# One tiling for near and far scores in attention, with masks and second norms on GpSimd and V's differences and routing steps on VectorE

## Chip, cores and metric

One core of one Trainium2 chip. The metric is device time in microseconds of one execution of the whole program; lower is better.

## The reference

```python
mod = (_silu(L0_c) @ L0_wmod).reshape(L0_c.shape[0], 6, 1, -1)
sa, ca, ga, sb, cb, gb = (mod[:, 0], ...)
ga = (2 * (ga >= 0) - 1) * jnp.maximum(jnp.abs(ga), 0.25)      # gb likewise
h = _layernorm(x, axis=-1) * (1 + ca) + sa
# attention: 16 heads of 64, 4 KV heads, on 4 x 1024 tokens of 128 features
scores = SOFTCAP * jnp.tanh((q @ k) * SCALE / SOFTCAP)         # SOFTCAP 30
mask = (j <= i) & (j > i - WINDOW)                             # WINDOW 128
o = softmax(where(mask, scores, -1e30)) @ v
x = x + ga * (o @ Wo.T)
h = _layernorm(x, axis=-1) * (1 + cb) + sb
# mixture of 8 experts, top 1, capacity C = tokens / 8 = 512
idx = jnp.argmax(softmax(h @ Wg), axis=1); loc = cumsum(one_hot(idx)) - 1
hidden = relu(h[rows of e] @ W1[e] + b1[e]); out = gate * (hidden @ W2[e] + b2[e])
x = x + gb * out                                               # (loc < C only)
```

## The kernel before, in words

4 batches of 1,024 tokens are cut into 32 tiles of 128 tokens (`BATCH_TILES` 8); two tiles make a block. `x` is normalised, turned (`turn_x`), split into a high and a low part and projected to Q, K and V in three passes per product. A tile needs its own keys and those of the tile before it in its batch; the first tile of a batch (`first(t)`) has no earlier one.

`score(t, h)` (TensorE, L478 to L489) makes 8 heads at a time: the tile's own keys go to the PSUM tensor `own` (2 banks), the keys of the tile before to two banks of `turns` (6 banks), in 16 matmuls of 32 keys with 512 down to 128 columns. `merge` (VectorE, L1352) copies the earlier tile's scores over own's by the triangle `before`, since a query sees each key slot in one of the two tiles. `weigh` and `expose` (ScalarE, L988 and L994) take tanh and exp into `PR`. `mask` (GpSimd, L1987) keeps of `PR` the part that belongs to the own tile, in `PM`.

Attention is linear in V: out = PR x V(t-1) + PM x VD, with VD = V(t) - V(t-1), made by `differ` on GpSimd (L1977). `sums` (L543) multiplies PR by ones. `attend` takes PR by V(t-1) for the first 64 queries and by VM for the other 64 (L521, all 128 keys deep), then PM by VD (L530, 64 keys deep, two row halves at once). VM is half V(t) and half V(t-1); SyncE copies it with 56 DMAs (`mix_v`, L326). ScalarE copies V out of PSUM (`keep_v`, L968).

After that, per tile: VectorE turns and inverts the sums and scales the output in two halves (`scale`, L1385), ScalarE takes the high part `OH` (L1001), GpSimd the low part `OL` (`low_o`, L1996), TensorE projects out and turns (`out_project`, `turn_y`), VectorE adds x and takes the moments (`add_x`, `measure2`, `gather2`), GpSimd the reciprocal deviation (`rstd2_of`, L2001 and L2003), VectorE normalises, modulates and shifts (L1408, L1416, L1420). TensorE turns that row (`turn_h2`) and scores the experts; VectorE finds the best one; GpSimd marks it (`mark`, L2012), adds it to the experts' counts (`add_seen`, L2022), numbers the slot, names the row and scatters it by an indirect DMA to `sorted_rows` (`scatter`, L2041). TensorE counts (`count`, L589, L590) between these steps, and needs `seen` of the tile before.

The expert stage (`place`, L814, to the end) starts with the rows of the last tiles, puts 512 rows an expert through W1 and W2 and scatters into the output.

The order of each engine's work is written out by hand: a loop over pairs of tiles and a longer list at both ends. Each PSUM bank has a table of tenants (`HOME`, `HOME_AT_ENDS`), and a tenant waits until the one before is read. At the end of the attention stage `run_between` (L602) puts 15 matmuls on zeros, 4,736 columns in all, between TensorE's steps.

## Time and profile before

| | |
|---|---|
| Three runs | 439.87, 441.22 and 441.91 us, median 441.22 |
| The profiled execution | 439.5 us, its span 437.8 us |
| TensorE busy | 418.3 us, 96% |
| VectorE, ScalarE busy | 288.8 us (66%), 296.9 us (68%) |
| GpSimd busy | 311.4 us (71%) |
| Head, to the first score | 15.9 us |
| Score of tile 8, 24, 28 begins | 90.8, 260.2, 301.3 us |
| Scatter of tile 28's rows is issued | 362.8 us |
| Expert stage | 366.3 us to the end |

In the trace an f32 matmul leaves two records, so "x32" at L530 are 16 matmuls. The end of a matmul's record holds its drain through the array, so the step from start to start, and not the duration, is the time one takes among others. Idle time is given in brackets with what ended it.

### The profile page before, as it was taken

The numbers are of one execution on the slowest core, as the hardware profiler recorded it, in microseconds if no ns is written. First come the engines' busy times: TensorE is split into PE (matmuls) and PEld (weight loads), VectorE is DVE, ScalarE is ACT, GpSimd is POOL, SyncE is SP. The second block draws the span as 40 slices with busy tenths as digits, with TensorE's granted clock in tenths as the row PEclk, the third lists the DMA queues.
The fourth block names the chain that finished last, engine by engine and source line by source line (L and its number), as shares of the span: only waits on it lengthen the run. The fifth ranks groups of instructions, "written<-read, shape, count | busy, mean of one in ns | idle before, by whom it ended". The sixth has DMA issues, their size and how long they took to land. (4 is left out here: it accounts for less than half of the span.)

```text
span 437.8 us, 15112 instructions
## 1 busy us (share of the span) xinstructions
PE 418.3 (96%) x5676; PEld 302.2 (69%) x5676; DVE 288.8 (66%) x884; ACT 296.9 (68%) x541; POOL 311.4 (71%) x496
## 2 busy tenths in 40 slices
PE   8989999999999999999999999999998998999992
PEld 4846666757676767576777767777664664789992
DVE  6485567666867686668585857676777665386751
ACT  4897676878695959776877787777677433645540
POOL 4267565758496979787979795889889974266663
PEclk9999999999999999999999999999999999999997
DMA  8087603000111020111212210302041152695010
GB/s 248 7 285 264 220 1 87 8 14 9 32 27 52 25 87 15 39 34 68 65 36 51 88 50 1 98 22 98 22 123 33 38 182 91 206 371 194 31 43 29
DMA packets 33023, 37.15 MB, mean 85 GB/s; under 512 B 3650, under 2 KB 29255, under 8 KB 32952
## 3 DMA queue, kind: packets, MB, share of 16 engines
q1 hardware_dynamic: 29448, 27.43, 20.4%
q0 software_dynamic: 3072, 8.37, 5.2%
q8 instruction: 46, 0.75, 0.7%
q10 hardware_dynamic: 432, 0.40, 0.4%
q14 instruction: 25, 0.20, 0.1%
...
## 5 line engine op out<-in xcount | busy, mean ns | idle before, releaser
L1352 DVE COPY_PREDICATED own<-before,turns 128x1024 f32<-128x1024 uint32 x56 | 68.5, 1223 | 52.0 <-PE turns L489 51.8
L988 ACT ACTIVATE PR<-own 128x1024 f32<-128x1024 f32 x64 | 65.7, 1027 | 33.6 <-DVE own L1352 32.2
L1996 POOL TENSOR_TENSOR OL<-O,OH 128x512 fp32r<-128x512 f32 x64 | 82.3, 1289 | 2.4 <-PE turns L530 1.1
L1987 POOL TENSOR_SCALAR_AFFINE_SELECT PM<-PR 128x1024 f32<-128x1024 f32 x64 | 69.7, 1098 | 17.0 <-ACT PR L994 16.6
L994 ACT ACTIVATE PR<-PR 128x1024 f32<-128x1024 f32 x64 | 67.1, 1054 | 0.1
L485 PE MATMUL own<-Q,K 64*32 64x128 f32 (+3 forms) x896 | 58.2, 436 | 1.7 <-ACT PR L988 1.4
L489 PE MATMUL turns<-Q,K 64*32 64x256 f32 (+3 forms) x896 | 57.7, 429 | 0.0
L1385 DVE TENSOR_TENSOR O<-turns,R 128x512 f32<-128x512 f32 x64 | 42.2, 685 | 11.4 <-PE turns L530 10.5
L2041 POOL DMA_INDIRECT sorted_rows<-PAY,slot_i x32 | 34.0, 1064 | 15.3 <-issue 10.2
L1001 ACT ACTIVATE OH<-O 128x512 fp32r<-128x512 f32 x64 | 40.0, 629 | 4.9 <-DVE O L1385 4.9
L489 PEld LDWEIGHTS turns<-Q,K 64*32 64x32 f32 x896 | 36.4, 107 | 9.3
L974 ACT ACTIVATE Q<-turns 128x512 f32<-128x512 f32 x64 | 37.8, 597 | 7.4 <-PE turns L411 6.5
L409 PE MATMUL turns<-XH,WqH 128*128 128x256 f32 x128 | 39.2, 306 | 0.1
L2001 POOL TENSOR_SCALAR var<-mv 128x1 f32<-128x1 f32 x32 | 6.2, 192 | 43.6 <-DVE mv L1404 42.2
L411 PE MATMUL turns<-XH,WqL 128*128 128x256 f32 x128 | 35.9, 281 | 0.0
L410 PE MATMUL turns<-XL,WqH 128*128 128x256 f32 x128 | 35.9, 281 | 0.0
L521 PE MATMUL turns<-PR,V 128*32 128x256 f32 x448 | 34.7, 380 | 0.0
L521 PE MATMUL turns<-PR,VM 128*32 128x256 f32 x448 | 34.5, 379 | 0.0
L557 PE MATMUL turns<-OH,WoH 128*128 128x256 f32 x128 | 32.7, 294 | 0.0
L1281 ACT ACTIVATE PM<-turns,b_col 128x512 f32<-128x512 f32 x28 | 19.3, 688 | 19.2 <-PE turns L411 19.1
L543 PE MATMUL turns<-PR,ones 128*32 128x512 f32 x224 | 29.8, 604 | 1.7 <-ACT PR L994 0.8
L558 PE MATMUL turns<-OH,WoL 128*128 128x256 f32 x128 | 31.1, 281 | 0.0
...
## 6 DMA issues: line engine op xcount, KB each, us to landing
...
```

The source lines that it names most:

```text
L409: pe.matmul(dst, wh, xh, start=True, stop=False)
L485: pe.matmul(own[lo:lo + B, a, :].rearrange("p (r n) -> p r n", n=P)[:, :, lo:P], keys(a, t, lo, lo + B), q(a, lo, P), start=True, stop=Tru ...
L489: last = pe.matmul(ps[lo:lo + B, a, :].rearrange("p (r n) -> p r n", n=P)[:, :, 0:lo + B], keys(a, t - 1, lo, lo + B), q(a, 0, lo + B), st ...
L521: last = pe.matmul(out_of(c, x, g), v[:, d], probabilities(PM if first(t) else PR, slice(0, P), g, c), start=(x == 0), stop=(x == 1 and fi ...
L974: act.activation(Q[:, k % Q_RING, 2 * n:2 * n + 2, :], bank["q", k, n].rearrange("p (c n) -> p c n", c=2), ACT.Copy).then_inc(q_kept[n], 1)
L988: act.activation(pr, own[:, :, :].rearrange("p a n -> p (a n)"), ACT.Tanh, scale=SCORE_SCALE).then_inc(tanhed, 1)
L994: act.activation(pr, pr, ACT.Exp, scale=SOFTCAP).then_inc(exped, 1)
L1001: act.activation(OH[:, t % 2, :, half], O[:, t % 2, :, half], ACT.Copy).then_inc(oh_done, 1)
L1352: dve.copy_predicated(own[:, :, :].rearrange("p a (r n) -> p (a r) n", n=P), before[:, :].bitcast(U32).unsqueeze(1).to_broadcast([P, 2 * R ...
L1385: dve.tensor_tensor(O[:, t % 2, :, half].rearrange("p c (r n) -> p c r n", n=HALF), bank["pv", t][:, :, half].rearrange("p c (r n) -> p c ...
L1987: pool.affine_select(out=PM[:, u % P_RING, :].rearrange("p (r n) -> p r n", n=P), in_=PR[:, u % P_RING, :].rearrange("p (r n) -> p r n", n ...
L1996: pool.tensor_tensor(OL[:, t % 2, :, half], O[:, t % 2, :, half], OH[:, t % 2, :, half].bitcast(F32), ALU.subtract).then_inc(ol_done, 1)
```

## The change

**Scores.** The 128 x 128 keys and queries of a tile are cut into halves of 64. A far pair (early keys with late queries or late keys with early queries) belongs wholly to one of the two tiles, a near pair to both by a triangle. `own` is laid out as far, near, near, far, so the near parts are the middle 512 of 1,024 columns (`NEAR`). `score` issues 24 matmuls instead of 16 for a later tile (16 instead of 4 for a first one), with the same number of columns for a later tile. `merge` and `mask` treat 512 columns instead of 1,024. `mask` is now a multiply by a 0/1 table `visible`, built at the start with three more GpSimd operations.

**Attention.** `sums` and the first half of the products are one function `attend` (L508, L519, L525), the rest is `correct` (L543, L552). All of it works on 64 keys a matmul, two row halves at once: 64 matmuls of 256 columns a later tile. VM, `mix_v` and its 56 DMAs are gone. The sums take two banks; the products of every tile have the same two banks (4 and 5), where odd and even tiles had different ones.

**Engines.** `keep_v` goes from ScalarE to VectorE; `differ`, `mark`, `name_row` and `number_slot` go from GpSimd to VectorE. `normalise2`, `modulate2` and `shift2` go from VectorE to GpSimd and keep their value in SBUF (`normed2`, in a free part of PM).

**Order.** All lists are written anew: projections of Q are issued up to a block earlier, the routing steps later, and `run_between` has 21 matmuls with 7,552 columns in place of 15 with 4,736. ScalarE splits the first weight of Q before it normalises x.

```diff
-        before = sb("before", [P, P])
-        earlier = YT[:, 0:P]
...
+        before, visible = sb("before", [P, HALF]), sb("visible", [P, HALF])
...
+        normed2 = PM[:, P_RING - 1, 2 * REP * HALF:2 * REP * HALF + 2 * P].rearrange("p (t n) -> p t n", t=2)
...
+        NEAR, NEAR_KEPT = slice(REP * HALF, 3 * REP * HALF), slice(0, 2 * REP * HALF)
+        def near(a):
+            return slice((1 - a) * REP * HALF, (2 - a) * REP * HALF)
+        def far(a):
+            return slice(a * REP * HALF, (a + 1) * REP * HALF)
 
...
+                if not first(t):
+                    n, ps = take_two("before", t, h)
+                for lo in range(0, P, B):
+                    there = HALF - lo // HALF * HALF
+                    for a in range(2):
+                        pe.matmul(heads(own[lo:lo + B, a, far(a)]), keys(a, t if first(t) or lo < HALF else t - 1, lo),
+                                  q(a, there, there + HALF), start=True, stop=True, tile_position=(HALF * a, lo))
+                for lo in range(0, P, B):
+                    here, from_ = lo // HALF * HALF, 0 if first(t) else lo % HALF
+                    for a in range(2):
+                        last = pe.matmul(heads(own[lo:lo + B, a, near(a)])[:, :, from_:HALF], keys(a, t, lo),
+                                         q(a, here + from_, here + HALF), start=True, stop=True, tile_position=(HALF * a, lo))
...
+                for lo in (B, 3 * B, 0, 2 * B):
+                    here, to = lo // HALF * HALF, lo % HALF + B
                     for a in range(2):
...
+                        last = pe.matmul(heads(ps[lo:lo + B, a, near(a)])[:, :, 0:to], keys(a, t - 1, lo),
+                                         q(a, here, here + to), start=True, stop=True, tile_position=(HALF * a, lo))
...
+                n, sm = take_two("sums", t)
                 if first(t):
                     pe.wait_ge(masked, 2 * t + 2)
                 else:
                     pe.wait_ge(exped, 2 * t + 2)
...
+                    for half in range(2):
+                        last = pe.matmul(sm[32 * g:32 * g + 32, half, near(half)], ones32[HALVES[half], :],
+                                         near_m(t, g, half) if first(t) else near_p(PR, t, g, half),
+                                         start=True, stop=first(t) and half == 0, tile_position=(HALF * half, 32 * g))
+                last.then_inc(near_summed, 1)
+                m, ps = take_two("pv", t)
+                if t % 2 == 0:
+                    pe.wait_ge(v_kept, t // 2 + 1)
+                for x in range(2):
+                    for g in range(KV):
+                        d = slice(g * D + 32 * x, g * D + 32 * x + 32)
+                        for half in range(1 if first(t) else 2):
+                            last = pe.matmul(out_of(ps, 1 - half, x, g), V[HALVES[half], (t - half) % V_RING, d], far_p(t, g, half),
+                                      start=(x == 0), stop=False, tile_position=(HALF * half, 32 * g))
+                last.then_inc(far_done, 1)
+                pe.wait_ge(near_summed, t + 1)
+                for g in range(KV):
+                    for half in range(1 if first(t) else 2):
+                        last = pe.matmul(sm[32 * g:32 * g + 32, 1 - half, near(1 - half)], ones32[HALVES[half], :], far_p(t, g, half),
+                                         start=False, stop=True, tile_position=(HALF * half, 32 * g))
...
-                freed[n] = sums_turned, t + 1
+                freed[n] = freed[n + 1] = sums_turned, t + 1
+                freed[m] = freed[m + 1] = scaled, 2 * t + 2
...
+            def correct(t):
...
+                ps = bank["pv", t]
+                pe.wait_ge(far_done, t + 1)
+                if not first(t):
+                    for x in range(2):
+                        for g in range(KV):
+                            d = slice(g * D + 32 * x, g * D + 32 * x + 32)
+                            for half in range(2):
+                                pe.matmul(out_of(ps, half, x, g), V[HALVES[half], (t - 1) % V_RING, d], near_p(PR, t, g, half),
+                                          start=False, stop=False, tile_position=(HALF * half, 32 * g))
+                    pe.wait_ge(masked, 2 * t + 2)
+                    pe.wait_ge(vd_done, later_tiles(t) + 1)
+                for x in range(2):
+                    for g in range(KV):
+                        d = slice(g * D + 32 * x, g * D + 32 * x + 32)
+                        for half in range(2):
+                            v = V[HALVES[half], t % V_RING, d] if first(t) else VD[HALVES[half], t % VD_RING, d]
+                            last = pe.matmul(out_of(ps, half, x, g), v, near_m(t, g, half), start=first(t) and half == 0 and x == 0,
+                                             stop=(x == 1), tile_position=(HALF * half, 32 * g))
+                last.then_inc(pv_done, 1)
+
+            def out_of(ps, c, x, g):
+                return ps[32 * g:32 * g + 32, c, x * 2 * P:(x + 1) * 2 * P]
...
-                freed[n] = h2_done, t + 1
+                freed[n] = x1_done, t + 1
...
-                dve.copy_predicated(own[:, :, :].rearrange("p a (r n) -> p (a r) n", n=P),
-                                    before[:, :].bitcast(U32).unsqueeze(1).to_broadcast([P, 2 * REP, P]),
-                                    bank["before", t, h].rearrange("p a (r n) -> p (a r) n", n=P)).then_inc(merged, 1)
+                if t == 1 and h == 0:
+                    dve.wait_ge(consts, MASKS)
+                dve.copy_predicated(own[:, :, :].rearrange("p a n -> p (a n)")[:, NEAR].rearrange("p (r n) -> p r n", n=HALF),
+                                    before[:, :].bitcast(U32).unsqueeze(1).to_broadcast([P, 2 * REP, HALF]),
+                                    bank["before", t, h].rearrange("p a n -> p (a n)")[:, NEAR].rearrange("p (r n) -> p r n", n=HALF)).then_inc(merged, 1)
...
+            def keep_v(k):
+                dve.wait_ge(v_projected, k + 1)
+                if k >= 3:
+                    dve.wait_ge(pv_done, 2 * k - 3)
+                r = 2 * k % V_RING
+                dve.tensor_copy(V[:, r:r + 2, :], bank["v", k].rearrange("p (t n) -> p t n", t=2)).then_inc(v_kept, 1)
...
+                dve.wait_ge(v_projected, t // 2 + 1)
+                dve.wait_ge(v_kept, (t + 1) // 2)
+                if t >= VD_RING:
+                    dve.wait_ge(pv_done, t - VD_RING + 1)
+                now = bank["v", t // 2].rearrange("p (t n) -> p t n", t=2)[:, t % 2, :]
+                dve.tensor_tensor(VD[:, t % VD_RING, :], now, V[:, (t - 1) % V_RING, :], ALU.subtract).then_inc(vd_done, 1)
...
-                pool.affine_select(out=PM[:, u % P_RING, :].rearrange("p (r n) -> p r n", n=P),
-                                   in_=PR[:, u % P_RING, :].rearrange("p (r n) -> p r n", n=P), compare_op=ALU.is_ge, fill=0.0,
-                                   base=0, pattern=[[0, 2 * REP], [1, P]], channel_multiplier=-1).then_inc(masked, 1)
+                pool.tensor_tensor(PM[:, u % P_RING, NEAR_KEPT].rearrange("p (r n) -> p r n", n=HALF),
+                                  PR[:, u % P_RING, NEAR].rearrange("p (r n) -> p r n", n=HALF),
+                                  visible[:, :].unsqueeze(1).to_broadcast([P, 2 * REP, HALF]), ALU.mult).then_inc(masked, 1)
...
+            def normalise2(t):
+                pool.wait_ge(rstd2_done, t + 1)
+                if t >= 2:
+                    pool.wait_ge(h2_done, t - 1)
+                pool.tensor_scalar(normed2[:, t % 2, :], PAY[:, t % PAY_RING, ROW_X:ROW_X + P], mv2[:, t, 0:1], rstd2[:, t:t + 1],
+                                  ALU.subtract, ALU.mult).then_inc(n_done, 1)
+
+            def modulate2(t):
+                n = normed2[:, t % 2, :]
+                pool.wait_ge(n_done, t + 1)
+                if t == 0:
+                    pool.wait_ge(mod_in, 16)
+                pool.tensor_tensor(n, n, mod[:, t // BATCH_TILES, 1, :], ALU.mult).then_inc(m_done, 1)
+
+            def shift2(t):
+                pool.wait_ge(m_done, t + 1)
+                pool.tensor_tensor(PAY[:, t % PAY_RING, ROW_H:ROW_H + P], normed2[:, t % 2, :], mod[:, t // BATCH_TILES, 0, :],
+                                  ALU.add).then_inc(h2_done, 1)
+
...
```

TensorE, one later tile of the steady loop, before (`turns` holds the results, P is 128):

```order
L543 MATMUL turns<-PR,ones 32x512 x4
L521 MATMUL turns<-PR,V 32x256 x4
L521 MATMUL turns<-PR,VM 32x256 x4
L521 MATMUL turns<-PR,V 32x256 x4
L521 MATMUL turns<-PR,VM 32x256 x4
L530 MATMUL turns<-PM,VD 32x256 x16
```

and now, from the first sums to the end of the next score:

```order
L508 MATMUL turns<-PR,ones 32x256 x8
L519 MATMUL turns<-PR,V 32x256 x16
L525 MATMUL turns<-PR,ones 32x256 x8
L543 MATMUL turns<-PR,V 32x256 x16
L552 MATMUL turns<-PM,VD 32x256 x16
L468 MATMUL own<-Q,K 32x256 x8
L473 MATMUL own<-Q,K 32x256 x2
L473 MATMUL own<-Q,K 32x4x32 x2
L473 MATMUL own<-Q,K 32x256 x2
L473 MATMUL own<-Q,K 32x4x32 x2
L481 MATMUL turns<-Q,K 32x256 x4
L481 MATMUL turns<-Q,K 32x4x32 x4
```

The deep matmuls on all 128 keys are gone, and the score follows the products at once.

GpSimd, steady loop, before, from a mask to a scatter:

```order
L1987 AFFINE_SELECT PM<-PR 128x1024 x2
L1977 TENSOR_TENSOR VD<-V 128x256
L2028 COPY PAY<-tok_id 128x1
L1996 TENSOR_TENSOR OL<-O,OH 128x2x256
L1987 AFFINE_SELECT PM<-PR 128x1024
L1963 TENSOR_SCALAR var<-mv 128x2
L1964 TENSOR_SCALAR minus<-mv 128x2
L1966 TENSOR_TENSOR rstd<-var,neg_half 128x2
L1969 TENSOR_TENSOR shift<-minus,rstd 128x2
L2041 DMA sorted_rows<-PAY,slot_i 32768x388
```

and now:

```order
L1983 TENSOR_TENSOR PM<-PR,visible 128x512
L1997 TENSOR_SCALAR var<-mv 128x1
L1999 TENSOR_TENSOR rstd<-var,neg_half 128x1
L2029 TENSOR_TENSOR seen<-seen,onehot 128x8
L2042 DMA sorted_rows<-PAY,slot_i 32768x388
L2029 TENSOR_TENSOR seen<-seen,onehot 128x8
L2005 TENSOR_SCALAR PM<-PAY,mv,rstd 128x128 x2
L2013 TENSOR_TENSOR PM<-PM,mod 128x128
L2017 TENSOR_TENSOR PAY<-PM,mod 128x128
L1983 TENSOR_TENSOR PM<-PR,visible 128x512
L2013 TENSOR_TENSOR PM<-PM,mod 128x128
L1992 TENSOR_TENSOR OL<-O,OH 128x2x256 x3
```

The mask has two operands and half the columns; the norm's steps (L2005, L2013, L2017) stand where `differ` and the naming stood, between masks and low parts.

GpSimd, the last operations up to the scatter of tile 28 (the last row of each), before:

```order
L2022 TENSOR_TENSOR seen<-seen,onehot 128x8
L2001 TENSOR_SCALAR var<-mv 128x1
L2003 TENSOR_TENSOR rstd<-var,neg_half 128x1
L2016 CAST slot_i<-slot 128x1
L2001 TENSOR_SCALAR var<-mv 128x1
L2003 TENSOR_TENSOR rstd<-var,neg_half 128x1
L2012 TENSOR_SCALAR onehot<-iota,top_at 128x8
L2041 DMA sorted_rows<-PAY,slot_i 32768x388
L2016 CAST slot_i<-slot 128x1
L2041 DMA sorted_rows<-PAY,slot_i 32768x388
```

and now:

```order
L1997 TENSOR_SCALAR var<-mv 128x1
L1999 TENSOR_TENSOR rstd<-var,neg_half 128x1
L1997 TENSOR_SCALAR var<-mv 128x1
L1999 TENSOR_TENSOR rstd<-var,neg_half 128x1
L2005 TENSOR_SCALAR PM<-PAY,mv,rstd 128x128
L2042 DMA sorted_rows<-PAY,slot_i 32768x388
L2013 TENSOR_TENSOR PM<-PM,mod 128x128
L2005 TENSOR_SCALAR PM<-PAY,mv,rstd 128x128
L2017 TENSOR_TENSOR PAY<-PM,mod 128x128
L2029 TENSOR_TENSOR seen<-seen,onehot 128x8
L2042 DMA sorted_rows<-PAY,slot_i 32768x388
```

Norm steps of later tiles stand between the last scatters, the marks and slot numbers have left.

## Rows read from the trace of the kernel before

**Rows 1.** The page: busy us, share, instructions; granted clock in 40 slices, in tenths.
```profile
PE 418.3 (96%) x5676; PEld 302.2 (69%) x5676; DVE 288.8 (66%) x884; ACT 296.9 (68%) x541; POOL 311.4 (71%) x496
...
PEclk9999999999999999999999999999999999999997
```

**Rows 2.** Windows: busy us of each engine (instructions), clock, DMA share, GB/s.
```profile
90.80:260.20 169.40, 168.27 (x2616) 120.05 (x2608) 117.74 (x373) 129.30 (x240) 131.53 (x213) 1.00 0.15 43
...
301.30:362.80 61.50, 58.91 (x834) 39.99 (x819) 42.45 (x159) 35.74 (x77) 53.12 (x91) 1.00 0.27 88
```

**Rows 3.** Timeline of TensorE, one later tile: start us, us, engine, line, operation.
```profile
203.03 1.07 PE L543 MATMUL turns<-PR,ones 128*32 128x512 f32 x8
...
205.75 1.09 PE L530 MATMUL turns<-PM,VD 64*32 64x256 f32 x32
206.64 0.63 PE L485 MATMUL own<-Q,K 64*32 64x512 f32 x12
...
207.85 0.39 PE L409 MATMUL turns<-XH,WqH 128*128 128x256 f32 x1
208.07 0.28 PE L410 MATMUL turns<-XL,WqH 128*128 128x256 f32 x1
208.19 0.28 PE L411 MATMUL turns<-XH,WqL 128*128 128x256 f32 x1
```

**Rows 4.** Timeline of TensorE in the head, with the idle time before each.
```profile
29.27 0.65 PE L485 MATMUL own<-Q,K 64*32 64x512 f32 x12 [0.45 <-ACT PR L988]
...
31.41 1.06 PE L543 MATMUL turns<-PR,ones 128*32 128x512 f32 x8 [0.82 <-ACT PR L994]
33.44 0.65 PE L485 MATMUL own<-Q,K 64*32 64x512 f32 x12 [0.97 <-ACT PR L988]
```

**Rows 5.** Groups of GpSimd by form: count, busy us, mean ns, idle before.
```profile
L1996 POOL TENSOR_TENSOR OL<-O,OH 128x512 fp32r<-128x512 f32 x64 | 82.3, 1289 | 2.4 <-PE turns L530 1.1 <-ACT OH L1001 1.0
...
L2041 POOL DMA_INDIRECT sorted_rows<-PAY,slot_i x32 | 34.0, 1064 | 15.3 <-issue 10.2 <-DMA Q<-sorted_rows 3.1 <-ACT PAY L1025 1.2
L1977 POOL TENSOR_TENSOR VD<-V 128x256 f32<-128x256 f32 x28 | 20.7, 740 | 0.1
...
L2012 POOL TENSOR_SCALAR onehot<-iota,top_at 128x8 bf16<-128x8 f32 x32 | 11.1, 346 | 3.1 <-DVE top_at L1433 2.4
...
L1958 POOL CAST earlier_b<-YT 128x128 bf16<-128x128 f32 x1 | 0.3, 283 | 0.0
```

**Rows 6.** Timeline of GpSimd in the steady stretch.
```profile
200.57 0.19 POOL L2001 TENSOR_SCALAR var<-mv 128x1 f32<-128x1 f32 x1
...
201.40 1.09 POOL L1987 TENSOR_SCALAR_AFFINE_SELECT PM<-PR 128x1024 f32<-128x1024 f32 x1
...
207.72 1.29 POOL L1996 TENSOR_TENSOR OL<-O,OH 128x512 fp32r<-128x512 f32 x1
208.96 0.55 POOL L2022 TENSOR_TENSOR seen<-seen,onehot 128x8 bf16<-128x8 bf16 x2
209.46 2.15 POOL L1987 TENSOR_SCALAR_AFFINE_SELECT PM<-PR 128x1024 f32<-128x1024 f32 x2
```

**Rows 7.** Timelines of GpSimd (first two rows) and TensorE at the stage's end.
```profile
360.32 1.11 POOL L2041 DMA_INDIRECT sorted_rows<-PAY,slot_i  x1 [0.17 <-issue]
...
362.78 0.98 POOL L2041 DMA_INDIRECT sorted_rows<-PAY,slot_i  x1 [1.13 <-issue]
...
361.35 0.60 PE L602 MATMUL own<-zeros 128*128 128x256 f32 x2
...
364.43 0.17 PE L589 MATMUL turns<-onehot,earlier_b 128*128 128x8 bf16 x1 [0.92 <-POOL seen L2022]
```

**Rows 8.** Groups by form of VectorE and ScalarE.
```profile
L1352 DVE COPY_PREDICATED own<-before,turns 128x1024 f32<-128x1024 uint32 x56 | 68.5, 1223 | 52.0 <-PE turns L489 51.8
...
L1416 DVE TENSOR_TENSOR turns<-turns,mod 128x128 f32<-128x128 f32 x32 | 9.4, 294 | 0.6
...
L994 ACT ACTIVATE PR<-PR 128x1024 f32<-128x1024 f32 x64 | 67.1, 1054 | 0.1
```

1574 lines of the change are left out of this document (720 added, 854 removed).

## The prediction

> **What bounds the kernel now.** I read the page's first two parts for the shares, the windows by stage, the timeline of TensorE in one steady stretch and in the head, then GpSimd's groups and timeline, and last the two engines' timelines at the end of the attention stage. TensorE is busy 96% of the span and its granted clock is full in every slice but the last [rows 1]; no other engine is above 71%. In the eight middle pairs of tiles (90.8 to 260.2 us) TensorE is busy 168.27 of 169.40 us while GpSimd is busy 131.53, or 16.4 of 21.2 us a pair [rows 2]. So there a microsecond counts only if it is TensorE's. In the stretch from the score of tile 28 (301.3) to its scatter (362.8) that turns: TensorE is at 58.9 of 61.5, part of it filler on zeros, GpSimd at 53.1 [rows 2]. In its last part TensorE runs filler on zeros (361.35) and waits 0.92 us for GpSimd's `seen` (364.43) [rows 7]. The expert stage can't start before the last scatters of rows, and GpSimd issues those (tile 28's at 362.78 [rows 7]). TensorE therefore owns the time up to about tile 28, GpSimd's list of work from there to the scatter. The head has three short stalls, 0.45, 0.82 and 0.97 us, each on ScalarE's tanh or exp [rows 4].
>
> **TensorE.** The score moves the same columns as before (5,120 a half tile), in 24 matmuls in place of 16; I cost it at nothing, as all of them keep one 32-column shape and the 16 of now take 1.21 us (206.64 to 207.85) [rows 3]. Attention: sums and PR by V and VM 2.72 us (203.03 to 205.75), PM by VD 0.89 to 206.64, together 3.61 [rows 3]. The change makes all of it 64 matmuls of 256 columns on half the rows, the shape of PM by VD, of which 16 take 0.89 with the change of shape ahead of them; four such sets with one change of shape for all are about 3.47. That is 0.14 less a tile, 3.4 over the 24 later tiles before tile 28 (4 more follow). Bounds: four times 0.89 is 3.56, a gain of only 0.05 a tile; nothing below 4 x 0.86 is likely, since the columns stay. The first tile of each of 4 batches gains some 0.2 each, 0.8 together. Leaving the half-row shape costs too: the first projection after a score starts 0.22 us before the second (207.85, 208.07), the second 0.12 before the third [rows 3], so an entry costs 0.1. Counted in the two orders, attention and score now follow each other without other work between, which takes the runs of half-row work from 66 to 56 (-1.0), but the projections and transposes are spread over 61 runs in place of 36 (+2.5). Part of the two overlaps (a run left is a run entered), so I take the net by tile 28 as -2.6, between -4.5 and 0.
>
> **Head.** Three stalls of 2.2 us in all [rows 4] have more projections ahead of them in the new order; the first projection is perhaps 0.5 later, because ScalarE splits a query weight before it normalises. I take -1.0, between -2 and +1.
>
> Score(28,0) then starts 3.6 us sooner, at 297.7 in place of 301.3 (the start of the second window in [rows 2]).
>
> **VectorE, ScalarE, SyncE.** VectorE's merge does half of its 1,024 columns (1,223 ns, 56 times [rows 8]), about 34 us less. It takes on keep_v (16 copies of 512 columns), differ (28, on 256) and three small steps a tile, and gives away the norm's three steps (the second 294 ns a tile [rows 8]): its total falls rather than rises. ScalarE loses keep_v. The 56 VM copies by DMA go; TensorE's timeline shows no wait for one ahead of PR by VM (203.03 to 205.75 without a gap [rows 3]). All of this costs and gives nothing while these engines are at 66 to 68% [rows 1]. If that cover went (VectorE now stands between v's projection and attention), the late piece would be keep_v behind a merge, half a microsecond a pair.
>
> **GpSimd, the term that decides.** No row shows a mask as a multiply of 512 columns by two inputs. From below: today's one-input mask of 1,024 columns takes 1.07 (two in 2.15 [rows 6]). From above, and nearest: low_o, two inputs of 512 columns, 1,289 ns, 1.24 us from start to start [rows 5, 6]. I take 1.24, so +0.17 a mask, 4 a pair. The two-input steps of the norm on 128 columns: the line from low_o's 512 over differ's 256 (740 ns) gives 0.47, and from start to start a little less; I take 0.43. Its first step has one input and two scalars out of columns. From below: a cast of 128 columns, 283 ns. But mark, one input and one such scalar, takes 346 ns for 8 columns alone, where var with constants takes 0.19 for one [rows 5, 6], so such scalars cost; I take 0.45, with 0.28 and 0.60 as bounds. That makes 1.31 a tile. What leaves a pair: differ 1.75 x 0.7, mark 2 x 0.35 [rows 5], and two one-column steps a tile at 0.19, together 2.7. A pair gets 0.7 + 2.6 - 2.7 = +0.6 and stands at about 17 busy of 21.2: hidden, as long as its order lets it be.
>
> At the end it is not hidden. After mask(28,0) the changed list, counted in its order, holds, up to the scatter of tile 28, 12 low_o at 1.24 = 14.9, 7 masks at 1.24 = 8.7, 8 second rstd at 0.83 (200.57 to 201.40 [rows 6]) = 6.6, 12 add_seen at 0.25 (208.96 to 209.46 for two [rows 6]) = 3.0, 11 scatters at 1.06 plus 0.17 of issue [rows 5, 7] = 13.6, 9 normalise at 0.45 = 4.0 and 16 steps of modulate and shift at 0.43 = 6.9: 57.7 us. Ahead of it: score 1.21, merge 0.65 (half of 1,223 ns), tanh and exp 2.1 (1,024 columns as now, exp 1,054 ns [rows 8]), 0.35 of hops, 4.3 together, and mask(28,0) itself, 1.2. With 1.0 for one forced wait on ScalarE's OH, as today at the last tile, the stretch is 64.2 us, against 61.5 now (301.3 to 362.8, the second window of [rows 2]): +2.7. So scatter(28) comes at 297.7 + 64.2 = 361.9 in place of 362.8: -0.9. The marks on VectorE shorten the last routing chain by 0.3. The filler grows by 6 matmuls and 2,816 columns; one of 256 takes 0.60 us with its tail (361.35 [rows 7]), so eleven such are 6.6 at most and some 5 with the tails overlapped, in a stretch where TensorE waits anyway; costed at nothing, and a rival below if that is wrong.
>
> The sum: -3.6 + 2.7 - 0.3 = **-1.2 us** on the profiled execution, which took 439.5 us with a span of 437.8. The median of the three runs is 441.22, so the forecast is **440.0 us**. About 0.5% (2.2 us) is what a measurement of this kernel can tell from no change.
>
> The price of modulate and shift rests on the line through two GpSimd rows; VectorE's own modulate of 128 columns takes 294 ns [rows 8], so the line puts GpSimd at 1.5 times that. The Trainium skill, GPSIMD Engine Reference, section 4.1 (Engine selection), puts elementwise add and multiply on VectorE and calls GpSimd about twice as slow with two inputs, near line rate with one. It speaks against this change, which hands GpSimd three kinds of two-input work; rival D is what it would make of it.
>
> **Rivals.** (A) GpSimd's new steps are cheap or well covered: the multiply costs no more than 1.07 and the head's stalls vanish (-2.2). The end stretch falls by 8 x 0.17 = 1.4 and the start by 1.2 more, which gives 437.4; with normalise at 0.28 also, 9 x 0.17 less, 435.9. For it: GpSimd's prices for 128 columns are interpolated. Against: low_o is a close neighbour of the multiply. (B) Slower: GpSimd becomes the bound already in the steady pairs. Its list is in-order, with masks behind norms that wait for rstd and for the tile's sum, and pv has one pair of banks for both parities now, so an attend waits for the scale of the tile before. If such a wait is 0.3 us a pair, 14 pairs lose 4.2, the 3.6 of gain is gone, and the end stretch still costs its 2.7: 439.5 + 4.2 - 3.6 + 2.7 - 0.3 = 442.5, and on the median's scale 444.2; at 0.45 a pair 446.3. It decides as soon as score(28,0) gains less than 2.4 us, for then +2.7 - 0.3 outweighs it. For it: GpSimd goes from 71% to a longer list in the same span, and it is the only engine that TensorE's attention needs late. Against: today it idles 4.7 us a pair [rows 2]. (C) The change does not do what it says at the end: the longer filler, not GpSimd, holds back the last counts. Filler stands between count and transpose on TensorE, so half of its extra 5 us would show: 442.5. (D) GpSimd takes twice VectorE's time for the two-input steps of the norm: 16 x (2 x 0.294 - 0.43) = 2.5 more at the end, 442.5. This is the rule named above from section 4.1; for it speaks only that today's two-input rows there are wide ones.
>
> **How the numbers follow.** The forecast case has 0.37, with a range of its own of 437.5 to 442.5; A 0.23, B 0.22, C 0.10, D 0.08. Faster by over 0.5% (below 439.0): all of A and 0.14 of the forecast case, 0.37. Slower (above 443.4): B, 0.02 of C, 0.02 of D and 0.01 of the forecast case, 0.27. Between: 0.36. The range takes in A down to 434.5, for stalls smaller still, and B up to 446.
>
> **What would show it.** Score(28,0) near 297.7; attend and correct of one tile 3.47 from start to end; the mask's multiply at about 1,290 ns; the norm's three steps at 400 to 480 ns each; from score(28,0) to the scatter of tile 28 some 64 us, GpSimd busy over 90% of it; TensorE's longest waits for GpSimd. Wrong would be: stalls of TensorE in the steady pairs for PM, OL or pv's banks (B), a full TensorE up to the last count (C), or a stretch of 60 us (A).

## The result, and the profile after

The changed kernel took **475.25 us** (median of 4 runs, 471.96 to 479.49) against 440.7 for the kernel before, run beside it: **1.0757 times as long, 95% interval 1.0658 to 1.0855**. One of the four runs fell in the slow state; the ratio, here and below, compares the means of the fast runs alone, which is why it isn't the quotient of the medians. The forecast was 440.0, with a range of 434.5 to 446. The profiled execution took 471.96, its span is 470.1.

The page of the kernel after, its shares and its slices, against [rows 1]:

```profile
PE 428.4 (91%) x8472; PEld 348.5 (74%) x8472; DVE 305.2 (65%) x928; ACT 289.3 (62%) x525; POOL 336.5 (72%) x471
...
PE   7999979999999999989899999899597969999992
...
POOL 5545555878886978979796989688579886246664
PEclk8999989999999999999999999999799989999997
```

TensorE is no longer busy throughout: 91% in place of 96. The windows of after say where; the first is that of [rows 2], the second runs from the last tanh to the scatter of tile 28:

```profile
core 0: us, PE busy (x) PEld busy (x) DVE busy (x) ACT busy (x) POOL busy (x), PEclk, DMA share, GB/s
90.80:260.20 169.40, 160.70 (x3814) 134.87 (x3822) 121.53 (x362) 118.78 (x214) 136.34 (x187) 0.99 0.10 30
...
365.20:395.00 29.80, 24.66 (x229) 16.20 (x228) 9.86 (x70) 8.80 (x25) 24.59 (x37) 0.94 0.35 116
```

In the same 169.4 us TensorE idles 8.7 where it idled 1.1 before. To compare kernels I cut each span at five marks that all have: the start of ScalarE's tanh for tile 8 and for tile 24 (first halves), the last tanh (tile 31, second half), the start of tile 28's scatter, the end. Between the first two lie eight pairs of tiles. Times in us, of the profiled executions, as differences of marks rounded to 0.1:

| kernel | to tile 8 | eight pairs | to last tanh | to scatter(28) | to the end | span |
|---|---|---|---|---|---|---|
| before | 94.4 | 168.0 | 80.6 | 19.8 | 75.0 | 437.8 |
| after | 97.5 | 177.7 | 90.0 | 29.8 | 75.1 | 470.1 |
| difference | +3.1 | +9.7 | +9.4 | +10.0 | +0.1 | +32.3 |

The loss is thus in three stages of some 10 us each, with 3.1 more ahead of them, and not in the expert stage. The costliest groups of VectorE and GpSimd in the changed kernel name a first suspect; these are rows of the page:

```profile
L1992 POOL TENSOR_TENSOR OL<-O,OH 128x512 fp32r<-128x512 f32 x64 | 81.8, 1290 | 17.5 <-ACT OH L1017 16.6
L1983 POOL TENSOR_TENSOR PM<-PR,visible 128x512 f32<-128x512 f32 x64 | 81.4, 1280 | 17.1 <-ACT PR L1010 16.8
...
L1359 DVE COPY_PREDICATED own<-before,turns 128x512 f32<-128x512 uint32 x56 | 38.6, 690 | 31.5 <-PE turns L481 31.4
...
L1459 DVE TENSOR_SCALAR onehot<-iota,top_at 128x8 bf16<-128x8 f32 x32 | 41.7, 1303 | 0.1
```

L1459 is `mark`, a comparison of 8 columns that the change moved from GpSimd to VectorE. On GpSimd it was 346 ns; here its mean is 1,303. Its own view (minimum, median and maximum) shows that this isn't its work:

```profile
L1459 DVE TENSOR_SCALAR onehot<-iota,top_at x32: 190/540/6254, 117.1 to 399.1; 128x8 bf16<-128x8 f32 x32
```

The timelines of GpSimd, VectorE and TensorE in one steady stretch show what it waits for:

```profile
203.93 1.29 POOL L1992 TENSOR_TENSOR OL<-O,OH 128x512 fp32r<-128x512 f32 x1
205.18 2.50 POOL L1983 TENSOR_TENSOR PM<-PR,visible 128x512 f32<-128x512 f32 x2
...
204.70 3.02 DVE L1459 TENSOR_SCALAR onehot<-iota,top_at 128x8 bf16<-128x8 f32 x1
207.63 0.68 DVE L1359 COPY_PREDICATED own<-before,turns 128x512 f32<-128x512 uint32 x1
...
208.37 0.38 PE L394 MATMUL turns<-XH,WqH 128*128 128x256 f32 x1 [1.27 <-DVE own L1359]
```

The mark begins while GpSimd is inside `low_o`, and ends at 207.72, 0.04 us after the two masks that follow end (205.18 + 2.50). The merge stands behind it on VectorE, tanh and TensorE's next projection behind the merge. Of the 32 marks 23 take over 0.25 us, and each of these ends 0.03 to 0.04 us after a GpSimd instruction does. Most wait out an unbroken run of them (the one of 6.25 us overlaps eight); a few, at 117.14, 317.09 and 374.74, get in between two that follow at once, so how long a run holds a mark isn't settled here. The other nine take 0.19 to 0.23: some meet an idle GpSimd, but three lie inside a one-column `rstd` step and one begins in a scatter, and these didn't hold them. TensorE's waits of after name the merge first:

```profile
PE turns L394 <- DVE own L1359: 5.9, 6, 1.3
PE turns L586 <- DVE PAY L1417: 5.3, 1, 5.3
PE turns L573 <- POOL OL L1992: 3.5, 2, 2.3
```

And GpSimd's groups give the norm's three steps, which I had put at 0.45, 0.43 and 0.43:

```profile
L2005 POOL TENSOR_SCALAR PM<-PAY,mv,rstd 128x128 f32<-128x128 f32 x32 | 25.4, 794 | 0.2
...
L2013 POOL TENSOR_TENSOR PM<-PM,mod 128x128 f32<-128x128 f32 x32 | 14.7, 460 | 0.2
L2017 POOL TENSOR_TENSOR PAY<-PM,mod 128x128 f32<-128x128 f32 x32 | 14.7, 458 | 0.9
```

### The profile page after: what moved, and what is told of

It is laid out like the page before. It is cut to its first block, busy times and chain, and to the rows that moved or that the text cites. A ratio compares the mean times of both kernels' runs of the same rounds, so it can differ in the third digit from the quotient of the medians.

```text
span 470.1 us, 20628 instructions
## 1 busy us (share of the span) xinstructions
PE 428.4 (91%) x8472; PEld 348.5 (74%) x8472; DVE 305.2 (65%) x928; ACT 289.3 (62%) x525; POOL 336.5 (72%) x471
## 4 chain that ended last, share of the span: by engine, by line
PE 67%; DVE 12%; issue 9%; POOL 7%; ACT 2%; DMA 1%; POOLq 0%; SPq 0%; DVEq 0%; ACTq 0%
PE own L468 6%; PE turns L899 5%; PE turns L394 5%; PE turns L519 5%; PE own L473 4%; PE turns L396 4%; PE turns L395 4%; DVE onehot L1459 4%; PE turns L552 4%; PE turns L508 3%; PE turns L543 3%; PE turns L525 3%; PE turns L481 3%; PE turns L573 2%; PE turns L568 2%
## 5 line engine op out<-in xcount | busy, mean ns | idle before, releaser
L1992 POOL TENSOR_TENSOR OL<-O,OH 128x512 fp32r<-128x512 f32 x64 | 81.8, 1290 | 17.5 <-ACT OH L1017 16.6
L1983 POOL TENSOR_TENSOR PM<-PR,visible 128x512 f32<-128x512 f32 x64 | 81.4, 1280 | 17.1 <-ACT PR L1010 16.8
L1359 DVE COPY_PREDICATED own<-before,turns 128x512 f32<-128x512 uint32 x56 | 38.6, 690 | 31.5 <-PE turns L481 31.4
L468 PE MATMUL own<-Q,K 64*32 64x256 f32 x1024 | 45.2, 393 | 4.3 <-issue 3.2
L394 PE MATMUL turns<-XH,WqH 128*128 128x256 f32 x128 | 38.8, 303 | 5.9 <-DVE own L1359 5.9
L473 PE MATMUL own<-Q,K 64*32 64x128 f32 (+1 forms) x1024 | 44.1, 339 | 0.0
L1459 DVE TENSOR_SCALAR onehot<-iota,top_at 128x8 bf16<-128x8 f32 x32 | 41.7, 1303 | 0.1
L1385 DVE STREAM_TRANSPOSE sumsT<-turns 128x512 f32<-128x512 f32 x32 | 22.9, 716 | 26.7 <-PE turns L525 26.7
L481 PE MATMUL turns<-Q,K 64*32 64x128 f32 (+1 forms) x896 | 38.5, 333 | 0.0
L519 PE MATMUL turns<-PR,V 64*32 64x256 f32 x960 | 35.9, 379 | 0.1
L552 PE MATMUL turns<-PM,VD 64*32 64x256 f32 x896 | 31.3, 376 | 0.0
L394 PEld LDWEIGHTS turns<-XH,WqH 128*128 128x128 f32 x128 | 24.3, 190 | 9.3 <-DVE own L1359 7.1
```

The costliest lines, as they stand in the source:

```text
L394: pe.matmul(dst, wh, xh, start=True, stop=False)
L468: pe.matmul(heads(own[lo:lo + B, a, far(a)]), keys(a, t if first(t) or lo < HALF else t - 1, lo), q(a, there, there + HALF), start=True, s ...
L473: last = pe.matmul(heads(own[lo:lo + B, a, near(a)])[:, :, from_:HALF], keys(a, t, lo), q(a, here + from_, here + HALF), start=True, stop= ...
L481: last = pe.matmul(heads(ps[lo:lo + B, a, near(a)])[:, :, 0:to], keys(a, t - 1, lo), q(a, here, here + to), start=True, stop=True, tile_po ...
L519: last = pe.matmul(out_of(ps, 1 - half, x, g), V[HALVES[half], (t - half) % V_RING, d], far_p(t, g, half), start=(x == 0), stop=False, til ...
L1459: dve.tensor_scalar(onehot[:, t, :], iota8[:, :], top_at[:, t, 0:1], None, ALU.is_equal).then_inc(one_done, 1)
```

## The experiments

Theories at the outset: (M) the marks hold VectorE; (G) GpSimd's longer list holds masks, low parts and counts back; (E) the order at the end holds the counts back. The runs went to several chips, on which the kernel before took 440.6 to 451.6; each ratio is against before on the same chip.

**1. The mark so that it doesn't wait.** The same comparison in the form that also writes out a sum:

```
-dve.tensor_scalar(onehot[:, t, :], iota8[:, :], top_at[:, t, 0:1], None, ALU.is_equal)
+dve.tensor_scalar(onehot[:, t, :], iota8[:, :], top_at[:, t, 0:1], 0.0, ALU.is_equal, ALU.add,
+                  accum_out=one_sum[:, :])
```

> The changed kernel with one edit: VectorE's mark has an accumulator output (the sum of its one-hot row, which nothing reads), at the same place with the same values. Theory L (lock): in the changed kernel each of the 32 marks (mean 1,303 ns, up to 6,254) ends 0.02 to 0.05 us after a GpSimd instruction ends, because this form of VectorE instruction, SBUF to SBUF with one input, can't start while GpSimd runs one; with the accumulator form it doesn't wait. Expected: mark 0.2 to 0.3 us with its read-out, 41.7 us of VectorE falling under 10, and a total of 440 to 448 us against 475.25. Theory G (GpSimd's list): the norms and two-input masks on GpSimd and the single pair of banks for the products slow the pairs, and the long marks are a symptom; then the total stays above 465 us whatever mark does.

Measured: 470.19 against 450.02, ratio 1.044 (1.0359 to 1.0522). The changed kernel itself, beside before on a chip of the same pace:

> The changed kernel itself, so that it stands beside the versions that follow on the same chip. Ratio to the kernel before 1.06 to 1.09 (1.0757 in the first runs). With theory L, the run with the accumulator form of mark (ratio 1.044 in its own comparison) keeps its distance of 2.5 to 3.5%.

Measured: 486.5 against 451.57, 1.0787 (1.0708 to 1.0867). The two versions with the mended mark and one more edit that ran on that very chip took 1.0516 and 1.0482 (steps 3 and 4), so the mark counts 2.7 to 3.1 points there. The mark's groups in the first of the two, the comparison and the read of the sum:

```profile
L1460 DVE TENSOR_SCALAR_CACHE_REDUCE onehot<-iota,top_at 128x8 bf16<-128x8 f32 x32 | 6.7, 209 | 0.3 <-issue 0.2
L1460 DVE DVE_READ_ACCUMULATOR onehot<-iota,top_at 128x1 f32 x32 | 2.7, 83 | 0.0
```

9.4 us of VectorE in place of 41.7, with the same neighbours on GpSimd, and 3.5 points of the ratio back, from one chip to another of the same pace (1.0787 to 1.044). Then the mark alone, in the kernel before:

> The kernel before with one part of the change alone: mark on VectorE right behind the search for the maximum's index. Theory L: GpSimd's instructions stand back to back less often here (131.5 of 169.4 us busy), so a mark waits 0.3 to 2 us; its mean is above 500 ns and the kernel is 2 to 15 us slower than 440.7, through the merges queued behind it. Theory G: mark takes 0.15 to 0.25 us and the kernel stays within 1 us of 440.7.

> The kernel before with mark on VectorE in the form with an accumulator output. Both theories: within 1.5 us of 440.7. If it is as slow as the run with the plain form, the wait is not one of the form, and something else about mark on VectorE (its place behind the index search, its semaphore) costs the time.

Measured: 1.0211 (1.0101 to 1.0321) with the plain form, 1.0023 (0.9984 to 1.0062) with the sum. The group rows, of the plain form and of the other:

```profile
L1437 DVE TENSOR_SCALAR onehot<-iota,top_at 128x8 bf16<-128x8 f32 x32 | 21.6, 675 | 1.1
```

```profile
L1438 DVE TENSOR_SCALAR_CACHE_REDUCE onehot<-iota,top_at 128x8 bf16<-128x8 f32 x32 | 7.1, 221 | 1.1
```

These two differ in the form of the mark alone and ran on one chip: one moved instruction of 8 columns a tile costs 2% by itself, between 1 and 3 by the interval. The Trainium skill, "SBUF — State Buffer", section "Who interferes with whom", states the rule: VectorE and GpSimd share one pair of ports by an exclusive lock, and a tensor_scalar, copy or cast of VectorE whose operands allow it can take it, but not the form that writes out its accumulator. By that rule both results follow, and the runs agree with it (675 ns the mean of the plain form, 221 that of the other).

**2. The mark back on GpSimd.** Two places in its list, ahead of the `add_seen` of the tile before, two tiles early and one tile early:

```
-dve: mark(t)
+pool: mark(t + 2), add_seen(t)        # second try: mark(t + 1), add_seen(t)
```

> The changed kernel with mark moved back to GpSimd (two a pair of tiles, put beside add_seen), everything else as changed. Theory L: 440 to 450 us, since nothing on VectorE waits for GpSimd's instructions any more and GpSimd gets 32 x 0.35 = 11 us more over the span, hidden in the pairs and at most 3 us at the end. Theory G: GpSimd's list gets longer, so slower still, above 475 us.

> Mark on GpSimd again, one tile later in its list than in the second run, which lost 90 us (ratio 1.24): there GpSimd idled 61.6 us at mark for VectorE's index search, its list held up masks and low parts behind it. Expected by theory L: GpSimd's wait at mark under 10 us and a ratio of 1.04 to 1.06, like the accumulator form plus 0.3 us a tile of GpSimd. If it still waits tens of us at mark, the order of the changed lists has no place for mark on GpSimd, and the run says nothing on the lock.

Measured: 1.2406 (1.2314 to 1.2499) and 1.0705 (1.0632 to 1.0778). GpSimd's first wait, then TensorE's, in the early place:

```profile
POOL onehot L2007 <- DVE top_at L1439: 61.6, 17, 5.2
```

```profile
PE turns L586 <- POOL PAY L1997: 45.6, 13, 4.7
```

GpSimd, in order, stands before the mark until VectorE has the index, and the norms queue behind it. In the later place it costs nearly as much as the lock did. So undoing this one move in the changed order isn't free; mending the form is better than either.

**3. The end.** First masks of tile 31 ahead of the four scatters on GpSimd, and `correct(31)` right behind `attend(31)`; then the same with `count(24)` ahead of them, VectorE's scale(31) right behind its sums, and no filler:

```
 pool: ... add_seen(24)
+mask(31, 0), scatter ..., mask(31, 1)
 scatter(20), scatter(21), scatter(22), add_seen(24), scatter(23)
-mask(31, 0), mask(31, 1)
```

> The changed kernel with mark in the accumulator form, and at the end two moves: GpSimd makes the two masks of the last tile before and among the four scatters that stood ahead of them, and TensorE issues correct(31) right behind attend(31) instead of after filler and routing steps. Theory E (order of the end): in the run with the accumulator form the last tanh is only 4.2 us later than in its neighbour on the same chip, but the last low_o 11.6 us later, since mask(31,1) waits behind four scatters (354.0 to 359.1 us) and correct(31) behind the mask and filler; so the total falls by 3 to 6 us against the accumulator form alone (ratio 1.031 to 1.038). Theory G (GpSimd's list is simply longer): the moves only permute its work, total within 1 us.

> The changed kernel with mark in the accumulator form and all 21 filler matmuls on zeros left out. Theory F (filler): in the chain of waits of the accumulator run from 357 us on, filler on zeros holds 16% of the chain and stands ahead of turns and counts; it was sized for routing steps that come sooner. Then the total falls by 2 to 6 us. Rival H: the filler keeps TensorE's granted clock up; without it the clock falls to half from 357 us on and into the expert stage, and the total stays or rises by up to 8 us.

> The accumulator run with the end rebuilt: the two masks of tile 31 ahead of the scatters, count(24) before and correct(31) right behind attend(31), VectorE's reciprocal and scale of tile 31 ahead of the routing steps of other tiles, no filler. Theory E (order of the end, as chains of waits): last low_o 6 to 8 us sooner than in the accumulator run (372.9 to about 366) and a total 5 to 9 us lower, ratio to the kernel before 1.025 to 1.033. Theory G (GpSimd's list as such) was contradicted by the cut norm already and would give no change.

> The kernel before without its 15 filler matmuls, as the measure for the filler of the changed kernel. Theory F: within 2 us of the kernel before. Rival H: 2 to 8 us slower, with granted clock down at the end of the attention stage or at the start of the expert stage.

Measured: reordered with filler 1.0516 (1.0465 to 1.0568); without filler 1.0353 (1.0295 to 1.0411), rebuilt 1.0332 (1.0286 to 1.0379); the kernel before without filler 1.0053 (1.0017 to 1.0089). Moving the masks brought the start of mask(31,1) from 5.7 us after the last tanh to 3.0, and the last `low_o` no sooner (20.2 us after it, 18.3 without the move). From the last tanh to the scatter of tile 28 the two without filler took 30.0 and 31.8 us. The order of the masks isn't what holds the end. 1.0516 is no gain over 1.044 either, though the two ran on different chips. The drop from 1.044 to 1.035 looks like the filler's; step 5 shows that it isn't.

**4. The norm on GpSimd.** A small cut first: normalise kept, its two other steps on one column each, so that modulation is left out of what is computed:

> The changed kernel with mark in the accumulator form, and the second norm's modulate and shift cut down to one column each, so that this part of the computation is left out: 0.52 us less of GpSimd a tile, 16.6 us over the span, semaphores as before. If GpSimd's list sets the end (11 tiles' norms stand there), the total falls by 4 to 7 us against the accumulator form alone; if chains of waits set it (norm steps lie in the last tiles' chain only), by 1 to 2 us; in the pairs nothing changes in either case.

Measured: 1.0482 (1.043 to 1.0534), no gain over 1.044, again on another chip. Then the norm alone, moved to GpSimd in the kernel before, right behind `rstd2`:

> The kernel before with one other part of the change alone: the second norm's three steps on GpSimd, each right behind rstd, at 0.80, 0.46 and 0.46 us (measured in the changed kernel). GpSimd gets 1.7 us a tile, 19.8 of 21.2 us a pair with its present 16.4. Theory G2: masks and low parts come later and TensorE waits in the pairs: 5 to 20 us slower. Rival: hidden in the pairs, and 2 to 5 us at the end, where three steps of 1.7 us in all stand in the last tile's chain in place of VectorE's 0.99.

Measured: 1.1176 (1.1116 to 1.1236). TensorE's first waits there:

```profile
PE turns L590 <- issue: 29.5, 16, 3.3
PE turns L563 <- POOL OL L1935: 7.7, 10, 1.7
```

L590 is there the first matmul of `count`, on the mark's onehot, which GpSimd makes: 29.5 us in 16 waits put down to "issue" (the profile names no releaser), and 7.7 for the low parts, also GpSimd's. In before's order the move costs 11.8%. Then the reverse, norm off GpSimd in the changed kernel. VectorE does it in two steps of two inputs and one scalar (with the mark mended; with filler, without, and with the end rebuilt):

```
+dve.scalar_tensor_tensor(normed2, PAY x, mean, mod 1, ALU.subtract, ALU.mult)
+dve.scalar_tensor_tensor(PAY h, normed2, rstd, mod 0, ALU.mult, ALU.add)
```

> The kernel is the changed one with the accumulator form of the mark (that took 1.044 of before), and the second norm's three steps taken off GpSimd: VectorE does it in two steps of two inputs and one scalar each. GpSimd loses about 1.7 us a tile, 55 us in all, and VectorE, at 58% busy, gains some 0.6 us a tile. GpSimd theory (the moved norms fill its in-order list, and masks, low parts and seen come late behind them): most of the 4.4 points go, 1.00 to 1.02, and score(28,0) comes 3 us or more sooner. Order theory (what is left is due to TensorE's new order, its 8,472 instructions in place of 5,676 and the late counts): 1.035 to 1.045, with GpSimd merely idle more. Between the two, at 1.025 to 1.035, each has a share.

> The same without the 21 stretches of filler on zeros. The changed kernel with the mark mended and no filler took 1.035. If GpSimd's norms hold the rest, this is the best of the family, 0.99 to 1.01; if the order holds it, 1.025 to 1.035.

> The same with the end rebuilt as well (masks of tile 31 ahead of the four scatters, VectorE's scale of tile 31 right behind its sums, no filler), which without the norms moved took 1.033. With a GpSimd that has little to do at the end, masks in that place should come within 5 us of the last tanh; if the end is bound by GpSimd's order this gives 0.5 to 1 point over the run before it, and if by the chain count, locate, scatter nothing.

Measured: 1.0993 (1.0932 to 1.1054), 1.1075 (1.1014 to 1.1136) and 1.0979 (1.0887 to 1.107). Outside every expectation. The two steps' own views:

```profile
L1436 DVE SCALAR_TENSOR_TENSOR PM<-PAY,mv,mod x32: 269/693/1462, 69.0 to 412.5; 128x128 f32<-128x128 f32 x32
```

```profile
L1441 DVE SCALAR_TENSOR_TENSOR PAY<-PM,rstd,mod x32: 333/352/1911, 70.5 to 412.9; 128x128 f32<-128x128 f32 x32
```

Alone they take 0.35 us; beside GpSimd at work up to 1.9, and the 37 above 0.45 us each end 0.15 to 0.16 us after a `low_o` or a mask of GpSimd does (one at 111.53 lasts 1.24, while a `low_o` ends 1.09 after its start). They have two inputs in SBUF. The rule of the Trainium skill, "SBUF — State Buffer", section "Who interferes with whom", has these wait as well, beside a GpSimd step that reads SBUF; the rows agree. Before's own norm goes through PSUM and shows nothing of it. Its normalise and its modulate:

```profile
L1408 DVE TENSOR_SCALAR turns<-PAY,mv,rstd x32: 335/412/416, 58.7 to 360.0; 128x128 f32<-128x128 f32 x32
```

```profile
L1416 DVE TENSOR_TENSOR turns<-turns,mod x32: 278/298/300, 60.7 to 361.0; 128x128 f32<-128x128 f32 x32
```

So the undo had the fault of the mark in it, and VectorE's in-order list, with these steps ahead of `differ` and the merges, was late besides (TensorE waits 7.0 us for `differ`). These three don't tell G's share.

To tell it, the norm was **left out**, so these kernels don't compute the reference: GpSimd takes one step of one column for the three, scores are taken from x1 and the rows for the experts hold zeros.

> The changed kernel with the mark in the accumulator form and filler kept (that took 1.044), with the second norm left out of the computation: GpSimd normalises, scales and shifts nothing, one step of one column stands for the three, and the expert scores are taken from the sum x1 itself; the rows handed to the experts hold zeros there. GpSimd's list is about 1.5 us a tile shorter, VectorE's and TensorE's lists are untouched. GpSimd theory (the norm's length holds the masks, low parts and counts behind it): 1.01 to 1.02, and from the last tanh to tile 28's scatter some 22 us in place of 32.9. Order theory (the late place of masks, counts and scatters in the lists, whatever the norm takes; cutting 0.5 us a tile gave nothing): 1.035 to 1.045 and 30 us or more. In between, 1.025 to 1.035, both share.

> The same without filler, against 1.035 for the changed kernel with the mark mended and no filler. GpSimd theory: 1.00 to 1.015. Order theory: 1.025 to 1.035, since counts 18 to 31 still stand behind the last attention in TensorE's list.

Measured: 1.0121 (1.0069 to 1.0173) with filler, 1.0169 (1.0119 to 1.0219) without. The last is to be held against 1.0353, the same lists with the norm, on the same chip: the intervals are apart, and **1.8 points are the norm's**. Filler seems worth some 0.5 here, as in the kernel before (1.0053, 1.0017 to 1.0089), but these two intervals overlap. The stretch from the last tanh to scatter(28), with norm and without, neither with filler:

```profile
346.20:376.20 30.00, 16.13 (x197) 12.21 (x197) 9.54 (x76) 8.82 (x25) 25.79 (x39) 0.71 0.34 115
```

```profile
346.10:372.00 25.90, 15.25 (x197) 10.90 (x196) 9.53 (x75) 8.82 (x25) 18.10 (x29) 0.84 0.36 120
```

GpSimd does 7.7 us less work and the stretch is 4.1 shorter. The five marks, all on the chip on which before took 440.6 to 441.8 (its own profile above is of a chip of the same pace):

| kernel | to tile 8 | eight pairs | to last tanh | to scatter(28) | to the end | span |
|---|---|---|---|---|---|---|
| before, no filler | 94.6 | 168.1 | 80.5 | 19.8 | 76.6 | 439.6 |
| mark mended, no filler | 99.2 | 168.0 | 79.0 | 30.0 | 78.0 | 454.2 |
| and norm left out | 100.9 | 165.2 | 80.0 | 25.9 | 77.2 | 449.2 |
| the same with filler | 97.7 | 165.2 | 79.5 | 24.8 | 76.1 | 443.3 |

**5. One more, and the chips.** The end rebuilt where the norm doesn't hide it:

> The kernel with the norm left out and no filler (1.017) and with the end's order rebuilt as in the run that took 1.033 against 1.035: masks of tile 31 ahead of the four scatters, count(24) ahead of the last attention, VectorE's scale of tile 31 right behind its sums. If the rest of the loss lies in that order, which the norm's steps had hidden before, this gives 1.003 to 1.010, and from the last tanh to tile 28's scatter 21 to 23 us in place of 25.9. If the rest lies elsewhere (the late counts, VectorE's list), it stays at 1.013 to 1.020.

Measured: 469.29 against 447.04, 1.0519 (1.046 to 1.0579). 3.5 points slower than the kernel that differs from it at the end alone, but on another chip. Their lists are the same up to tile 24. The window of the eight pairs, first on the chip of 1.0169, then here:

```profile
100.90:266.10 165.20, 164.56 (x4000) 140.25 (x4000) 108.84 (x402) 124.84 (x227) 123.05 (x172) 1.00 0.11 34
```

```profile
97.20:271.50 174.30, 171.84 (x4001) 140.96 (x4000) 108.72 (x402) 124.80 (x227) 123.91 (x172) 1.00 0.11 32
```

The same instructions on every engine, the same busy time on VectorE, ScalarE and GpSimd within 1 us, the same granted clock, and 9.1 us more. TensorE's and GpSimd's timelines at one scatter, on the first chip (TensorE) and here (TensorE, then GpSimd):

```profile
159.33 1.07 PE L553 MATMUL turns<-PM,VD 64*32 64x256 f32 x32
160.19 0.64 PE L469 MATMUL own<-Q,K 64*32 64x256 f32 x16
```

```profile
157.08 1.47 PE L553 MATMUL turns<-PM,VD 64*32 64x256 f32 x32
158.68 0.73 PE L469 MATMUL own<-Q,K 64*32 64x256 f32 x16
...
157.37 1.08 POOL L2018 DMA_INDIRECT sorted_rows<-PAY,slot_i  x1 [0.17 <-issue]
```

From `correct` to the score it is 0.86 us there and 1.60 here, and the pause in between ends 0.2 us after the scatter does. For each scatter between 120 and 280 us I took the longest time between the starts of two matmuls, from 0.8 us ahead of the scatter's end to 0.2 behind it. In the ten profiles of changed kernels from the four chips on which before took 447 to 452, the median of those 10 to 14 is 0.46 to 0.52 us; in five from chips on which it took 440.6 to 441.8 it is 0.17 to 0.21. A window of the same length 1 to 3 us earlier gives 0.17 or 0.18 on both sorts. Where the matmuls of the two windows above can be laid side by side, the slower chip loses 8.3 us, 7.7 of them from 0.6 us ahead of a scatter's end to 0.5 behind it. The pauses keep to the scatter, not to a matmul: in the kernel of 1.0482 they begin after matmuls 2805 and 3327, in that of 1.044 after 2820 and 3342. In the kernel before it is 0.19 on the one sort and 0.27 to 0.31 on the other, no more than in windows away from its scatters. So on some chips, in this order, TensorE pauses for about half a microsecond with GpSimd's scatters. In the changed order these fall among the half-row matmuls of attention and score; that it needs those is only suggested, and what on the chip does it stays open. It mends the reading of steps 1 to 4: 1.044, 1.0482 and 1.0516 stand on chips with pauses (eight pairs 173.7, 174.8 and 174.1), 1.035 and 1.033 on one without (168.0 and 168.9). With filler taken at 0.5, the changed kernel with the mark mended would take some 1.030 there; that is worked out, not run. Of E this run says only that the end didn't get shorter either: 28.7 us from the last tanh to scatter(28).

No version tried beats the kernel before. The one that computes the reference and comes nearest is before with its mark in the sum form on VectorE, 1.0023, no different from it.

## Why the prediction was wrong, step by step

**"Three small steps a tile" on VectorE, "all of this costs and gives nothing"**: this is the step that failed. I costed VectorE by its share (66 to 68%), found the work light, and never asked whether a step of VectorE can be held up by GpSimd's steps. Of the three steps two have one column (136 and 143 ns, they never wait); the mark has 8. It costs 2.7 to 3.5 points where before took 450 to 452 (step 1), and on chips without pauses all 9.7 us of the eight pairs and 11.0 of the stretch behind them: 177.7 and 90.0 with the plain mark, 168.0 and 79.0 with the mended one. It does nothing to the stretch from the last tanh to scatter(28) (29.8 and 30.0). Even the sentence on what goes wrong if VectorE's cover is gone named only keep_v, half a microsecond a pair. TensorE then did wait in the steady pairs, as rival B (444.2) says, but for VectorE's merge behind a mark (4.6 of the waits in the eight pairs, at L394), by a mechanism that no rival had.

**TensorE, -2.6 by tile 28**: right in kind, and as a saving of TensorE larger than I said. With mark and norm out of the way eight pairs take 165.2 in place of 168.0, or 0.35 a pair, where -2.6 over 14 pairs is 0.19. Attend and correct of a later tile take 3.45 to 3.48 us from start to start, where before takes 3.61: 0.13 to 0.16 where I said 0.14. The first tile of a batch takes 3.02 in place of 2.87, so it loses 0.15 where I had it gain 0.2. Nothing of the saving arrives at the end: score(28,0) starts at 315.4 in after and, with the mark mended, at 305.3, in place of the 297.7 forecast.

**Head, -1.0**: the first tanh came 2.2 us sooner (15.3 against 17.5), then the order lost more: tile 8's tanh is 3.1 late in after, and 3.3 with the mark mended and the norm left out. TensorE's timeline there has one pause of 3.06 us in a score at 59.57, with no releaser, and all fifteen kernels of this order have one at 59.5 to 61.8 (2.4 to 3.1 us); no kernel of before's order has one of that length in the head. In each a transfer of the instruction queue q8, 1.0 to 1.1 us long, overlaps the pause. SyncE's eight writes of `empty_row` to `sorted_rows`, 776 KB each, were issued at 24.6 to 46.1 in before; in the new order they are issued at 46.4 to 57.4 and fill the DMA engines just then, and right behind the pause the granted clock of after is 0.50 for 3.4 us. In after, from 47 to 70, then those 3.4 us, and 47 to 70 in before:

```profile
47.00:70.00 23.00, 20.31 (x449) 15.99 (x430) 11.07 (x27) 10.48 (x16) 12.69 (x16) 0.93 1.04 342
62.50:65.90 3.40, 3.26 (x42) 2.43 (x42) 0.78 (x2) 0.06 (x1) 1.01 (x2) 0.50 1.06 355
```

```profile
47.00:70.00 23.00, 22.00 (x391) 15.45 (x391) 14.73 (x30) 16.32 (x24) 14.16 (x19) 1.00 0.36 111
```

A pause of 3 us is as much as the 3.1 that tile 8 is late. That the moved writes hold up the instructions, and these TensorE, fits every one of the fifteen profiles, but before has a q8 transfer at 60.5 too, with idle DMA engines and no pause, and no run put the writes back: it isn't shown. The prediction has no term for where SyncE's writes stand.

**GpSimd**: mask 1,280 ns, I took 1,240 from start to start, and modulate and shift 460, I took 430: right. Normalise 794, where I took 0.45 and bounded by 0.60: a mis-sized term, 0.34 us a tile too small. Its nearest row was the mark's 346 ns, of 8 columns. "Hidden in the steady pairs" was wrong as well: the norm costs 2.8 us in the eight pairs (168.0 to 165.2), 0.35 a pair, which is the 0.3 to 0.45 of rival B and as much as TensorE had saved. B's price was right, and I gave it 0.22; its mechanism was not. It had TensorE wait for masks, low parts or pv's banks behind the norms. With the mark mended TensorE waits for none of these in the eight pairs. It waits for the norm's own result, shift2's row, which `turn_h2` turns:

```profile
PE turns L587 <- POOL PAY L1997: 2.0, 5, 0.7
```

These 2.0 us are most of the 2.8, and with the norm left out the line is gone.

**The end, 64.2 in place of 61.5**: from score(28,0) to the scatter after takes 79.6 us (315.4 to 395.0), with GpSimd busy 62.6 of them, 79% where I said over 90. From tile 28's tanh it is 76.9 against 58.4, so +18.5 where I had +2.7. Without filler it is 68.4 with the mark mended, +10.1 over before without filler (58.3), and 65.0 with the norm left out as well, +6.7 (with filler 63.2, +4.8). I had summed GpSimd's list as if it ran without a break but one. In the 30.0 us of the window above GpSimd is busy 25.8, VectorE 9.5, TensorE 16.1: the stretch is a chain of engines that wait for one another in turn, tile by tile, and every longer step lengthens it. What holds the last 5 to 7 us is open; it isn't the place of the masks of tile 31 (step 3), and the run meant to tell more fell on a chip with pauses.

**Rivals.** A (437.4) fell with normalise's 794. C isn't borne out: taking the filler away cost 0.5 points in the kernel before and 0.5, with overlapping intervals, with the norm left out; it gave none. Filler alone was not taken from the changed kernel as it stands. D (442.5) took twice VectorE's time for the steps of two inputs; they take 1.56 times (460 to 294). It is the one-input step that is 1.95 times VectorE's (794 to 407). The Trainium skill, "GPSIMD Engine Reference", section 4.1 (Engine selection), has one-input work on GpSimd near line rate. The row of 794 ns (one input, two scalars out of columns) doesn't agree, and the measurement decides.

The parts, in points, on chips without pauses: 7.6 in all; the mark some 4.5 (from 1.0757 to 1.0353, and an estimated 0.5 for the filler that the second lacks; the two ran at different times, each beside before at 440.6 or 440.7), the norm 1.8, and 1.2 left with both gone. Those are 5.5 us of span: +3.3 to tile 8 (the pause above is the likely piece), -2.8 in the eight pairs, -1.1 to the last tanh, +5.0 at the end, +1.1 behind it. On chips with pauses the mark counts 2.7 to 3.5. Pause and lock seem to overlap: from the one sort of chip to the other the eight pairs grow by 2.1 us with the plain mark (177.7 to 179.8) and by 5.7 with the mended one (168.0 to 173.7).
